# Cached values gathered by rows on GpSimd for every head group, staged pages kept for keys alone

## The reference

```python
k_c = k_cache[block_table]; v_c = v_cache[block_table]      # 16 pages of 32 keys per batch, 8 key heads of 128
scores = einsum('bqhd,bkhd->bhqk', q, k_all) * SCALE         # 32 query heads, 512 cached + 128 new keys
probs = softmax(where(valid, scores, -1e30))
o = einsum('bhqk,bkhd->bqhd', probs, v_all)
x = x + o @ Wo.T
```

## Time and profile before

| what | value |
|---|---|
| median of 3 runs | 1293.17 us (1291.05 to 1293.62) |
| time of the profiled execution | 1294.06 us |
| its span | 1291.2 us |
| granted TensorE clock, mean | 0.999 |
| TensorE busy | 1269.8 us, 98% |
| VectorE, ScalarE, GpSimd busy | 1017.5, 840.3, 932.9 us |
| DMA traffic | 265.66 MB |
| chain of waits that ended last | PE 87%, DVE 6%, POOL 4%, ACT 1%, issue 1%, DMA 1% |

### The profile page before, as it was taken

One profiled execution on the slowest core, in us unless ns is written; L12 is line 12 of the kernel. 1 busy time (PEld: TensorE's weight loads), 2 busy tenths in 40 slices (PEclk: granted clock), 3 DMA queues, 4 the chain that ended last, 5 costly groups with the idle time before them and its releaser, 6 DMA issues.

```text
span 1291.2 us, 25180 instructions
## 1 busy us (share of the span) xinstructions
PE 1269.8 (98%) x7068; PEld 1110.1 (86%) x7068; DVE 1017.5 (79%) x2054; ACT 840.3 (65%) x2217; POOL 932.9 (72%) x1173
## 2 busy tenths in 40 slices
PE   9999999999999999999999999999999999999999
PEld 8777888888888888888888888888888888888887
DVE  6887888878888888887888888888788887658546
ACT  7666566767676667766766767676766685535444
POOL 7889888878897888888888888887887822424211
PEclk9999999999999999999999999999999999999999
DMA  6788679967986897689669957996765364363532
GB/s 218 235 250 258 210 216 270 260 171 211 271 234 172 244 270 206 183 262 270 162 183 288 274 154 209 269 263 168 206 164 167 122 195 141 122 211 127 187 123 81
DMA packets 260027, 265.66 MB, mean 206 GB/s; under 512 B 139776, under 2 KB 211072, under 8 KB 249216
## 3 DMA queue, kind: packets, MB, share of 16 engines
q1 hardware_dynamic: 254208, 228.77, 61.6%
q0 software_dynamic: 5760, 36.18, 8.3%
HBM read 182.57 MB, written 82.31 MB: 205 GB/s over the span
## 4 chain that ended last, share of the span: by engine, by line
PE 87%; DVE 6%; POOL 4%; ACT 1%; issue 1%; DMA 1%; SPq 0%; DVEq 0%; POOLq 0%; ACTq 0%
PE ps L65 26%; PE ps L66 25%; PE ps L67 25%; PE ps L1364 6%; DVE at_pT_lo L1031 2%; POOL at_probs L634 1%; PE ps L1406 1%; DVE ds_lo L1031 1%; DVE at_probs L1083 1%; PE ps L2319 1%; DMA q_rows<-at_q_turned_rows 0%; ACT at_pT_hi L766 0%; DVE xres L1100 0%; PE ps L1340 0%; POOL at_inv_rms L591 0%
## 5 line engine op out<-in xcount | busy, mean ns | idle before, releaser
L819 ACT ACTIVATE at_probs<-at_probs,at_neg_max 128x640 f32<-128x640 f32 x256 | 210.1, 822 | 124.9 <-DVE at_neg_max L1083 124.9
L634 POOL TENSOR_SCALAR at_probs<-at_probs,at_row_inv 128x640 f32<-128x640 f32 x256 | 215.8, 853 | 104.3 <-DVE at_row_inv L1093 99.7
L1083 DVE CUSTOM_DVE_ANT_0 at_probs<-ps,at_mask,at_inv_rms 128x640 f32<-128x640 f32 x256 | 223.6, 880 | 19.5 <-PE ps L67 17.5
L65 PE MATMUL ps<-ds_hi,x_hi 128*128 128x512 f32 (+1 forms) x564 | 192.9, 342 | 1.0 <-POOL ds_hi L610 0.5
L67 PE MATMUL ps<-ds_hi,x_lo 128*128 128x512 f32 (+1 forms) x564 | 192.1, 341 | 0.0
L65 PE MATMUL ps<-at_kT_hi,ds_lo 128*128 128x320 f32 x512 | 159.9, 312 | 4.7 <-DVE at_pT_lo L1031 1.3
L766 ACT ACTIVATE at_pT_hi<-ps 128x512 fp32r<-128x512 f32 x196 | 111.4, 603 | 76.6 <-PE ps L1364 73.3
L67 PE MATMUL ps<-at_kT_hi,ds_lo 128*128 128x320 f32 x512 | 158.1, 309 | 0.0
L66 PE MATMUL ps<-at_kT_lo,ds_lo 128*128 128x320 f32 x512 | 158.1, 309 | 0.0
L1031 DVE TENSOR_TENSOR at_pT_lo<-ps,at_pT_hi 128x512 fp32r<-128x512 f32 x196 | 128.5, 683 | 22.1 <-ACT at_pT_hi L766 21.9
L65 PE MATMUL ps<-at_pT_hi,at_v_hi 128*128 128x512 f32 x320 | 127.2, 397 | 6.3 <-DVE xres L1100 4.3
(11 more groups left out here) (226 smaller groups left out, 3620.6 us busy)
## 6 DMA issues: line engine op xcount, KB each, us to landing
turned_rows<-at_turned SPq DMA_DIRECT2D x62, 512.0 KB
at_pT_raw<-turned_rows SPq DMA_DIRECT2D x248, 128.0 KB
kT_pages<-shared SPq DMA_DIRECT2D x16, 1024.0 KB, 5.6
q_rows<-at_q_turned_rows SPq DMA_DIRECT2D x248, 64.0 KB
at_qT_raw<-q_rows SPq DMA_DIRECT2D x62, 256.0 KB
kv_raw<-kT_pages SPq DMA_DIRECT2D x60, 256.0 KB, 4.2
v_pages<-shared SPq DMA_DIRECT2D x14, 1024.0 KB, 5.7
kv_raw<-v_pages SPq DMA_DIRECT2D x56, 256.0 KB, 3.4
```

What stands on the lines that cost most here:

```text
L65: pe.matmul(out, l_hi, r_hi, start=first, stop=False)
L634: pool.tensor_scalar(probs[:, h, :], probs[:, h, :], row_inv[:, h:h + 1], 1.0, ALU.mult, ALU.mult).then_inc(probs_done, 1)
L819: act.activation(probs[:, h, :], probs[:, h, :], ACT.Exp, bias=neg_max[:, h:h + 1], scale=-1.0, accum_out=row_sum[:, h:h + 1]).then_inc(ex ...
L1083: dve.tensor_tensor_reduce(out=probs[:, h, :], in0=slot(h), in1=mask[:, b, :], scale=inv_rms[b % 2][:, h:h + 1], scalar=3.0e38, op0=ALU.ad ...
```

## The change

Values are gathered by rows in every group. GpSimd issues one `gather` of 256 KB for each batch, from `v_cache` straight into `v_raw`; `v_pages`, its 14 stores, its 56 loads and the 14 gathers of value half pages are gone. Only keys are staged, in 2 steps per group (bodies 2 and 3, by `STAGE_AT`) in place of 4. The table `VALUES_AT` puts the gathers: in groups 1 to 6 batches 3 and 4 in body 1, 5, 6 and 7 in bodies 2, 3 and 4, the next group's 0 and 1 in body 6 and 2 in body 7; group 0 has those of bodies 6 and 7 beside its own, group 7 those of bodies 1 to 4. That is 56 gathers more. Once per group `next_keys` advances `key_idx` to the next head by two small instructions, at the end of body 5. SyncE no longer issues or waits for anything of the values.

```diff
+        STAGE_AT = (2, 3)
+        VALUES_AT = {1: (3, 4), 2: (5,), 3: (6,), 4: (7,), 6: (B, B + 1), 7: (B + 2,)}
...
             def stage_pages(g, step):
...
-                wait_apart(pool, kv_stored, STAGED_FIRST + g * 64 + step * 16, passed)
-                if step % 2 == 0:
...
-                cache = (kT_rows, v_cache.rearrange("a h (t r) d -> (a h t) (r d)", t=2))[step % 2]
+                wait_apart(pool, kv_stored, STAGED_FIRST + g * 32 + step * 16, passed)
+                pool.tensor_scalar(page_row[:], page_row[:], 1.0, None, ALU.add).then_inc(page_step, 1)
+                wait_apart(pool, page_step, g * 4 + step * 2 + 6, passed)
+                pool.tensor_copy(page_idx[:], page_row[:]).then_inc(page_step, 1)
+                wait_apart(pool, page_step, g * 4 + step * 2 + 7, passed)
...
+            def gather_values(g, b):
+
+                wait_apart(pool, v_cache_done, upto(g, b, 1) - 1, passed)
+                gather(b % B, v_rows, v_raw, v_loaded)
+
+            def next_keys(g):
+
+                for j in range(2):
+                    wait_apart(pool, v_loaded[j], values_count(g, B - 2 + j), passed)
+                pool.tensor_scalar(key_row[:], key_row[:], float(PSIZE // LC), None, ALU.add).then_inc(key_step, 1)
+                wait_apart(pool, key_step, g * 2 + 2, passed)
+                pool.tensor_copy(key_idx[:], key_row[:]).then_inc(key_step, 1)
+                wait_apart(pool, key_step, g * 2 + 3, passed)
...
                     def stage():
-                        if first and 2 <= b < 6:
-                            stage_pages(g, b - 2)
-                        if not first and not last and 1 <= b < 5:
-                            stage_pages(g, b - 1)
+                        if not last and b in STAGE_AT:
+                            stage_pages(g, STAGE_AT.index(b))
...
+                    if b in VALUES_AT and not (first or last) or first and b >= B - 2 or last and b < B - 3:
+                        for v in VALUES_AT.get(b, ()):
+                            gather_values(g, v)
                     if started:
                         stage()
...
+                    if b == B - 3 and not last:
+                        next_keys(g)
```

More of the change, by code:

```diff
@@ L82, in make_identity, with attention @@
                        pattern=[[-1, P]], channel_multiplier=1).then_inc(step, 1)
-def attention(nc, block, x, xT, ints, floats, wq, wkv, wo, k_cache, kT_cache, v_cache, kT_pages, v_pages, ident, xres, wq_raw, shared, dense, loads, turned_rows, q_rows):
+def attention(nc, block, x, xT, ints, floats, wq, wkv, wo, k_cache, kT_cache, v_cache, kT_pages, ident, xres, wq_raw, shared, dense, loads, turned_rows, q_rows):
     with ExitStack() as ctx:
@@ L219, in attention @@
         kT_loaded = [sem(f"kT_loaded{j}") for j in range(2)]
-        vp_loaded = [sem(f"vp_loaded{j}") for j in range(2)]
+        key_step = sem("key_step")
         k_loaded = [sem(f"k_loaded{j}") for j in range(2)]
@@ L274, in upto, with values_count @@
             return g * (B * per) + (b * per + k)
+        def values_count(g, b):
+            return g * (B // 2 * 16) + (b // 2 + 1) * 16
         def by_row(g):
@@ L393, in store_pages @@
             def store_pages(g, step):
-                wait_apart(sp, kv_staged, STAGED_FIRST + g * 64 + step * 16 + 16, passed)
-                pages, half = (kT_pages, v_pages)[step % 2], slice(step // 2 * ROW, (step // 2 + 1) * ROW)
-                sp.dma_start(pages[bass.ds((g + 1) * (B * NPP), B * NPP), half], kv_stage[:]).then_inc(kv_stored, 16)
+                wait_apart(sp, kv_staged, STAGED_FIRST + g * 32 + step * 16 + 16, passed)
+                half = slice(step * ROW, (step + 1) * ROW)
+                sp.dma_start(kT_pages[bass.ds((g + 1) * (B * NPP), B * NPP), half], kv_stage[:]).then_inc(kv_stored, 16)
             def store_turned(g, b):
@@ L456, in group @@
                         store_turned(g, b)
[L457 to L463, removed]
+                    if not last and b - 1 in STAGE_AT:
+                        store_pages(g, STAGE_AT.index(b - 1))
                     if not by_row(g) and not last and b == 1:
@@ L2414, in _, with stages @@
                 adapter(i)
-def stages(nc, t, kT_pages, v_pages, out):
+def stages(nc, t, kT_pages, out):
     with ExitStack() as ctx:
@@ L2431, in stages @@
                   t["L0_cond_Wo"], t["L0_cond_k_cache"], t["kT_cache"], t["L0_cond_v_cache"],
-                  kT_pages, v_pages, ident, xres, staging, shared, dense, loads, turned_rows, q_rows)
+                  kT_pages, ident, xres, staging, shared, dense, loads, turned_rows, q_rows)
         early = loads.early = swiglu_buffers(ctx, nc, shared, dense)
@@ L2492 @@
     out = nc.dram_tensor("out", (B, S, DM), F32, kind="ExternalOutput").ap()
-    kT_pages, v_pages = (nc.dram_tensor(n, (HK * B * NPP, 2 * ROW), F32).ap() for n in ("kT_pages", "v_pages"))
-    stages(nc, t, kT_pages, v_pages, out)
+    kT_pages = nc.dram_tensor("kT_pages", (HK * B * NPP, 2 * ROW), F32).ap()
+    stages(nc, t, kT_pages, out)
     r = run_bass_kernel_spmd(nc, [arrays], core_ids=[0])
```

25 lines of the change are left out of this document (7 added, 18 removed).

## The result

| | median | runs | ratio to before, 95% |
|---|---|---|---|
| before | 1292.58 us | 6 (1291.05 to 1293.62) | |
| after | 1298.87 us | 6 (1297.33 to 1301.82) | 1.0048 (1.0036 to 1.0059) |

The change costs 6.3 us. The forecast was 1291.8 us with a range of 1289.4 to 1295.8, so it is wrong in sign and outside its range. What came is its rival 1, the loop overflows, and somewhat more than the top of that rival's price (1297.7 us).

The account below looks back on a forecast made before the run. TensorE, busy 98% of the span, was taken to bound the kernel. Terms of -1.23 and -0.11 us in group 0 and 0 elsewhere, rounded to -1.4, gave 1293.17 - 1.4 = 1291.8 us, range 1289.4 to 1295.8.

Parts of the forecast that it names:

- rival 1: Loop: from about 1.7 us per gather TensorE waits in bodies 3 and 4; up to +5.9 us, 1291.8 to 1297.7; 18%.
- What bounds the kernel: Whole kernel: TensorE busy 98% of the span, 15.28 us per loop body; removing waits wins at most some 21 us.
- Body 5 of group 0, -1.23 us: Group 0, body 5: without the value step GpSimd's next work starts 1.23 us earlier, shrinking TensorE's wait by that.
- The marks: Group 0, body 5: L616 starts 0.04 us after the gather; VectorE's split at about 129.4 takes some 2.3 us.
- rival 2: Group 0, end of body 5: VectorE's split gets through after L610, not L605, closing both waits; -2.2 to -3.0 us; 10%.
- Bodies 3 and 4 of group 0, -0.11: Group 0: key step moves from body 4 to body 3; GpSimd ends body 4 0.11 us earlier, reaching TensorE in body 5.
- the 0.97 us of the key step: Group 0, body 3: GpSimd's sequence with a key step taken as 0.97 us longer than with a value step.
- The loop, 0 us: Groups 1 to 6: gathers at 1.25 us just fit GpSimd's room before the row sums; 0 us, at most +5.9.
- the 0.45 us of body 1: Loop, body 1: GpSimd's lateness with two gathers if each takes the upper bound of 1.95 us.
- `next_keys`, 0.6 us and covered: Loop, ahead of body 6: two index instructions take about 0.6 us, within 3.5 us of room for two gathers; 0.
- Group 7 and SyncE, 0: Group 7, body 1: two gathers (2.50 us) fit an idle 2.59 us; SyncE loses 70 issues, TensorE unaffected; 0.
- The cover, 0.66 us: Loop: VectorE's idle time in the body behind absorbs at least 0.66 us of GpSimd's lateness.

Follow-up runs that it names:

- the control: The changed kernel run once more with no further edit, beside three follow-up runs: 1299.02 us, 1.0055 of the kernel before.

## Why the prediction was wrong, by its steps

- **What bounds the kernel**: held. TensorE's own 15.28 us is a floor, and the 29.4 MB brought nothing.
- **Body 5 of group 0, -1.23 us**: right in size, 1.30 measured alone. The marks came too: L616 starts at 128.88, 0.03 us behind the gather (0.04 forecast, though the step's own row gives 129.74 - 129.72 = 0.02), and VectorE's split took 2.23 us (2.3 forecast).

```profile
128.88 1.31 POOL L616 TENSOR_TENSOR ds_hi<-at_wkv_raw,ds_hi 128x512 fp32r<-128x512 f32 x1
130.15 1.29 POOL L611 TENSOR_TENSOR ds_lo<-staging,ds_hi 128x512 fp32r<-128x512 f32 x1
```

```profile
129.77 2.23 DVE L1038 TENSOR_TENSOR ds_lo<-staging,ds_hi 128x512 fp32r<-128x512 f32 x1
```

  This also settles rival 2: the split ends at 132.00, 0.56 us behind the end of L611 (131.44), not of L616 (130.19), so it was again held past two GpSimd instructions, as in the earlier trace rows, where it ended 0.71 behind the second. The Trainium skill (SBUF — State Buffer, Who interferes with whom) has a VectorE instruction with two SBUF inputs and a GpSimd instruction that reads SBUF contend for one exclusive port pair, which both rows bear out; that VectorE gets its turn after one instruction, as I had read it, neither shows.
- **Bodies 3 and 4 of group 0, -0.11**: the sum held, the place didn't. The forecast put the 0.97 us of the key step nowhere on TensorE; it stands in body 4 (16.08 to 17.05), and body 5 gave as much more back (21.31 to 18.99, not to 20.0). Bodies 3 to 5 together: 54.33 before, 53.05 in the control, -1.28 for the forecast -1.34.
- **The loop, 0 us**: this is the step of the prediction that failed, at the words "a gather waits for values that were split long ago". That is true of the first gather in bodies 1 and 6 (0.16 us). In bodies 2, 3, 4 and 7 the table asks for batch b+3, whose buffer the split of batch b+1 frees, and that split is the instruction right in front, on the same engine. The forecast had the price of just that case in hand (0.85, upper bound 1.95 a gather), had the threshold (1.7) and the place (the first waits of bodies 3 and 4), and gave it 18%. The way to be sure was to write for each body which split its gather waits for, and where it stands in the order: a line of arithmetic on `upto(g, b, 1) - 1`. The sign that it had named for the rival, a gap of 0.85, came as 0.82. Measured at 1.92 in bodies 2 and 3, the overflow took 1.2 us a group, where the rival had 0.98 as its price. Its working was not right in all terms: the 0.45 us of body 1 didn't come, since the pair there costs 0.16 + 1.10 + 0.30 + 0.95 = 2.51; what it left out is that a late normalising takes 1.84 us and not 0.80 in five of the six groups, though the kernel before had such a row (112.16 in the earlier trace rows). The edit that makes the waits older gives back 746.81 - 739.91 = 6.9 us.
- **`next_keys`, 0.6 us and covered**: both wrong. It takes 1.09 us with its two short waits, and it stands not in body 6's room but ahead of it, before the low parts of keys and queries for which VectorE and TensorE wait: 0.3 us of TensorE time a group.
- **Group 7 and SyncE, 0**: held; from body 3 of group 7 on, the traces differ only by the last body's two lengths.
- **The cover, 0.66 us**: it was there, and more. In group 3 of the kernel before, VectorE's transposes (L1118) start 1.94 us ahead of bodies 3 and 4. In the kernels with gathers in the loop, bodies whose transposes start 0.9 us ahead or more lose 0.05 us at most (0.16 once), those at 0.64 us ahead lose about 0.3, at 0.47 about 0.46, at 0.29 about 0.65; one body lies far off (1.09 at 0.25). So 1.0 us of lateness was covered there, and what went beyond it came out of TensorE in full.

## What to carry to other kernels

For each wait in a moved or added instruction, write down which instruction signals it and how far back in the order it stands; if it is the one just ahead on the same engine, charge the gap of the nearest such row. Where a body of the loop just fits, the gap decides, and the cure can be free, as here with an older partner. Look also at what a late instruction will run into: here being late cost GpSimd a second microsecond. Count small index arithmetic ahead of an indirect DMA as part of that DMA, and compute it in a body that has room: here that brought 2.7 us by the medians, more than taking 29 MB off the queues.

## What the runs showed of the hardware

- A gather of 128 rows of 2 KB holds GpSimd 1.10 us, or 0.95 behind another DMA (in group 0 up to 1.45 at times). Ahead of it stand 0.15 to 0.18 us where its wait is old, 0.30 behind another DMA, and, where it waits for the instruction just ended on GpSimd, 0.82 in the loop but 0.28 in group 7. There the same pair of instructions reads:

```profile
952.96 1.26 POOL L636 TENSOR_TENSOR at_v_lo<-kv_raw,at_v_hi 128x512 fp32r<-128x512 f32 x1
954.50 1.11 POOL L524 DMA_INDIRECT kv_raw<-in_L_cond_v_cache,at_key_idx  x1 [0.28 <-POOL at_v_lo L636]
```

  In group 7 the count that is waited for is a constant; in the loop it comes from a register, and `wait_apart` puts a semaphore increment between wait and DMA. The key step shows the same two values (0.28 in group 0, 0.81 in the loop). Which of the two parts the 0.54 us belong to wasn't tried.
- GpSimd's late start feeds on itself. The first normalising of a body takes 0.80 us where it starts on time. In all fourteen traces, every one outside group 7 that takes 1.79 to 1.86 us starts inside VectorE's split of the turned probabilities (two inputs in SBUF) and ends 0.57 to 0.60 us behind the end of that split. Some that start inside it take 0.94 to 1.37 us only; what decides between the two isn't clear from the rows. One that starts ahead of the split keeps its time (0.81 us, row of 455.36 above), and the split behind it takes 1.43 us, against 1.29 elsewhere.
